# Decoder layer on one core: the last residual sum and the output store of each block in two halves

## The chip, the core and the metric

The kernel runs on one core of a Trainium2 chip. The core has five engines that run side by side, each with a queue of its own: TensorE (PE; its weight loads are listed apart as PEld), VectorE (DVE), ScalarE (ACT), GpSimd (POOL) and SyncE (SP), which here only issues transfers. They wait for each other through semaphores. What counts is the device time of one launch in microseconds (us).

## What is computed

A decoder layer on x of 4 x 1024 tokens with 256 features, in float32. Cut to what matters:

```
x = x + mixer(layernorm(x))              # a state-space scan over time, a projection, its own residual
x = x + cross_attention(ctx, ctx, layernorm(x))       # 16 heads, 64 keys
h = silu(s1 * (z @ w1.T)) * (s2 * (z @ w2.T))         # z = layernorm(x), 256 -> 1024
h = gelu(sh1 * (h @ h1.T)); h = gelu(sh2 * (h @ h2.T))
x = x + s3 * (h @ w3.T)                               # 1024 -> 256
```

The change is in the last line: the sum of x and the feed-forward output, and the store of the result.

## The kernel before

The first part (to about 200 us) is the mixer. The second part, which the change touches, goes over the 4096 tokens in 8 blocks of 512 (`NBLK`, `BLK`). Seven of them run in a loop on every engine (`Fori(0, NBLK - 1)`), the eighth is written out behind it. While the feed-forward part of block i is computed, the attention part of block i + 1 is woven into it; the eighth block has no attention part beside it.

A weight matrix stays in SBUF; an activation is kept as a high and a low part (`hi`, `lo`), so that each product is two matmuls of 128x128 by 512 columns. TensorE (line 1094 on) does per block eight groups of gated products (`gated`, line 1057), 16 groups of hidden products (line 1070), two groups with `w3T` (`last`), and `turn_out` (line 1087): eight transposes that bring the output, which lies with features on the partitions in `sg`, back to tokens on the partitions in the PSUM buffer `pair[2]`. The transposes of feature half k = 0 come first, those of k = 1 behind a wait for ScalarE's second evacuation (`o_ev`, line 775). In `pair[2]` token tile m takes the columns m * 256 to (m + 1) * 256, so its first 512 columns are complete when tiles 0 and 1 of k = 1 are turned.

VectorE's order is written out by hand. At the end of a block it computes the low part of the next block's input (`z_lo`, line 884), then waits for `o_t` and for `xr_in` (the residual rows, loaded by SyncE into `xr` a whole block ahead) and adds (line 954). Right behind the add, in the next trip of the loop, come the statistics of the attention part (`stats`, lines 834 to 841) and then the gated product of group 0 (line 918), for which ScalarE has computed `sg` (line 759). TensorE needs that product's semaphore `v_rdy` before gated group 2, since the groups take turns in two PSUM buffers.

SyncE's order in a trip: load `xr` for block i (line 618), store x2 of block i + 1, load the rows and values of block i + 2, store the output of block i (`out_store`, line 620). After the eighth block it waits for the store, and all engines meet at a barrier (line 1320). Behind it a second program stands that runs only for weights that need it; here each engine reads a flag and branches past it.

Of the kernel before, what the change touches and what calls it, by code (L numbers as in the profile page):

```python
# [29 lines left out]
ALU = mybir.AluOpType  # L30
# [12 lines left out]
BLK = 512  # L43
NBLK = TOK // BLK
TPB = BLK // P
EPS = 1e-5
DH = DM // P
# [488 lines left out]
def layer_program(nc, ctx, a, t):  # L536
    m = mixer_parts(nc, ctx, a, t)
    take = {"a": t["zone_a"], "c": t["zone_c"], "d": t["zone_d"], "s": t["zone_s"]}

    def sb(name, shape, where, dt=F32):  # L540
        size = -(-4 * math.prod(shape[1:]) // 32) * 32
        at, take[where] = take[where], take[where] + size
        return nc.alloc_sbuf_tensor_at(name, shape, dt, offset=at)

    def sem(name):
        return ctx.enter_context(nc.semaphore(name))
# [6 lines left out]
    xr = sb("xr", [P, TPB * DM], "c")  # L553
# [16 lines left out]
    warm = sb("warm", [P, 2], "s")  # L570
    bit_row = bits[0:1, 0:P]
    pair, ident, scl = t["pair"], t["ident"], t["scl"]
# [7 lines left out]

    names = ("h2_in", "xbo_in", "mk", "k_rdy", "v_rdy2", "vb0",
             "stat2", "aggr2", "var_rdy", "rstd", "nat_rdy", "nat_t", "x1b", "sc_ps", "mx", "sub", "exped", "summed", "rcp", "p_rdy",
             "p_t", "t_ev", "av", "wo_ps", "x2a", "x2_rdy", "z_hi", "z_lo", "mm", "sg_rdy", "v_rdy", "hi", "lo", "o_ev", "o_t", "fin1", "fin",
             "x1_in", "v_in", "xr_in", "x2_st", "out_st", "step_v2", "step_s2", "checked", "folded", "col_st", "row_in", "flagged", "warm", "step_g2")
    S = {n: sem("f_" + n) for n in names}

    def blk_rows(d, i):
        return d[bass.ds(i, 1)].rearrange("a p m -> (a p) m")
# [7 lines left out]
    @block.sync  # L596
    def _(e):
        m["sync"](e)

        def attn_loads(j):  # L600
            if not (isinstance(j, int) and j == 0):
                e.wait_ge(S["x2_st"], 16 * j)
                e.sem_inc(S["step_s2"], 1)
                e.wait_ge(S["nat_rdy"], 8 * j)
                e.dma_start(x1t[:, :], blk_rows(x1d, j)).then_inc(S["x1_in"], 16)
            e.wait_ge(S["av"], 2 * j)
            seq = j // (T // BLK)
            for d in range(2):
                e.dma_start(vblk[KEYS * d:KEYS * (d + 1), :], a["ctx"][bass.ds(seq, 1)].rearrange("a s d -> (a s) d")).then_inc(S["v_in"], 16)

        def x2_store(j):
            e.wait_ge(S["x2_rdy"], j + 1)
            e.dma_start(blk_rows(x2d, j), x1t[:, :]).then_inc(S["x2_st"], 16)

        def res_load(i):
            e.wait_ge(S["x2_st"], 16 * i + 16)
            e.wait_ge(S["out_st"], 16 * i)
            e.dma_start(xr[:, :], blk_rows(x2d, i)).then_inc(S["xr_in"], 16)

        def out_store(i):  # L620
            e.wait_ge(S["fin"], i + 1)
            e.dma_start(blk_rows(a["out"], i), xr[:, :]).then_inc(S["out_st"], 16)
        e.wait_ge(m["h_scan"], NOCT)
        attn_loads(0)
        e.dma_start(xbo[:, :], a["xb"].partition_broadcast(P)).then_inc(S["xbo_in"], 16)
        for i in range(1, NBLK):
            m["x1_store"](e, i)
        e.wait_ge(m["x1_st"], 16 * (NBLK - 1))
        e.wait_ge(m["w_d"], 80)
        e.dma_start(t["h2"].bitcast(F32), t["dh2"]).then_inc(S["h2_in"], 16)  # L630
        x2_store(0)
        attn_loads(1)
        with e.Fori(0, NBLK - 2) as i:
            res_load(i)
            x2_store(i + 1)
            attn_loads(i + 2)
            out_store(i)
        res_load(NBLK - 2)
        x2_store(NBLK - 1)
        out_store(NBLK - 2)  # L640
        res_load(NBLK - 1)
        e.wait_ge(S["folded"], 2)
        e.dma_start(t["flag_col"], most[:, :]).then_inc(S["col_st"], 16)
        e.wait_ge(S["col_st"], 16)
        e.dma_start(bit_row, t["flag_col"].rearrange("p o -> o p")).then_inc(S["row_in"], 16)
        out_store(NBLK - 1)
        e.wait_ge(S["out_st"], 16 * NBLK)

    @block.gpsimd
    def _(e):  # L650
# [175 lines left out]
    def _(e):  # L826
# [4 lines left out]
        def stats(n):  # L831

            for m in range(TPB):
                e.bn_stats(st[:, m, :], x1t[:, m * DM:(m + 1) * DM]).then_inc(S["stat2"], 1)
            e.wait_ge(S["stat2"], 4 * n + 4)
            e.wait_ge(S["nat_rdy"], 4 * n)
            e.sem_inc(S["step_v2"], 1)
            for m in range(TPB):
                e.bn_aggr(mv[:, m, :], st[:, m, :]).then_inc(S["aggr2"], 1)
            e.wait_ge(S["aggr2"], 4 * n + 4)  # L840
            e.tensor_scalar_add(ve, mv[:, :, 1], EPS).then_inc(S["var_rdy"], 1)  # L841
# [44 lines left out]
        def low(i, n, dst):  # L886

            e.wait_ge(S["hi"], 24 * i + (n + 1))
            e.tensor_tensor(dst[1][:, n % HC, :], vb[:, n % 2, :], dst[0][:, n % HC, :], ALU.subtract).then_inc(S["lo"], 1)  # L889
# [20 lines left out]
        def body(i, attn):  # L910
            j = i + 1
            if attn:
                e.wait_ge(S["x1_in"], 16 * j)
                stats(2 * j)
            for m in range(HC):
                e.wait_ge(S["sg_rdy"], 8 * i + (m + 1))
                e.wait_ge(S["lo"], 24 * i + max(m - 1, 0))
                e.scalar_tensor_tensor(vb[:, m % 2, :], pair[m % 2][:, 512:1024], sc2[:, m:m + 1], sg[:, m % 2, :],  # L918
                                       ALU.mult, ALU.mult).then_inc(S["v_rdy"], 1)
                if m == HC - 1:  # L920
                    e.wait_ge(S["lo"], 24 * i + m - 1)
                    low(i, m - 1, h1)
                    low(i, m, h1)
                if attn and m == 1:
                    normed(2 * j)
            if attn:
                maxima(j, 0)
                shifted(j, 0)
            for s in range(2 * HC):
                low(i, HC + s, h2 if s < HC else h1)  # L930
                if attn and s in TURN and s != TURN[3]:
                    shifted(j, TURN.index(s) + 1)
                if attn and s + 1 in TURN and s + 1 != TURN[3]:
                    maxima(j, TURN.index(s + 1) + 1)
                if attn and s + 2 in TURN:
                    normalised(j, TURN.index(s + 2))
                if attn and s == 13:
                    residual(j)
                    stats(2 * j + 1)
                if attn and s == 14:  # L940
                    normed(2 * j + 1)
                checks = CHECK if attn else LAST_CHECK
                if s in checks:
                    checked(i, checks.index(s))
                if not attn and s == LAST_CHECK[2] + 1:
                    folded()
                if not attn and s == FLAG_AT:
                    e.wait_ge(S["row_in"], 16)
                    e.tensor_reduce(t["flag"][:, :], bit_row, AX.X, ALU.max).then_inc(S["flagged"], 1)
            if attn:  # L950
                z_lo(j)
            e.wait_ge(S["o_t"], i + 1)
            e.wait_ge(S["xr_in"], 16 * i + 16)
            e.tensor_tensor(xr[:, :], pair[2][:, :], xr[:, :], ALU.add).then_inc(S["fin"], 1)
        m["x1_add"](e, 0)
        e.wait_ge(m["x1a"], 1)
        stats(0)
# [29 lines left out]
    def _(e):  # L987
# [18 lines left out]
        def scores(j, u):  # L1006
            if u == 0:
                e.wait_ge(S["t_ev"], 7 * j + 1)
                e.wait_ge(S["k_rdy"], 2 * j + 2)
                if not isinstance(j, int):  # L1010
                    e.wait_ge(S["fin"], j - 1)
            else:
                e.wait_ge(S["sub"], 4 * j + u)
            h = u // 2
            for b in range(2):
                tile = 2 * (u % 2) + b
                for g in range(2):
                    ins = e.matmul(pair[2][:, g * BLK + b * 256:g * BLK + (b + 1) * 256], qa[64 * g:64 * g + 64, h, tile * P:(tile + 1) * P],  # L1018
                                   kblk[64 * g:64 * g + 64, h * 256:(h + 1) * 256], start=True, stop=True)
            ins.then_inc(S["sc_ps"], 1)  # L1020
# [66 lines left out]
        def turn_out(i):  # L1087
            for k in range(DH):
                e.wait_ge(S["o_ev"], 2 * i + (k + 1))
                for m in range(TPB):  # L1090
                    ins = e.transpose(pair[2][:, m * DM + k * P:m * DM + (k + 1) * P], sg[:, k, m * P:(m + 1) * P], ident[:, :])
            ins.then_inc(S["o_t"], 1)

        def body(i, attn):
            j = i + 1
# [273 lines left out]
```

## Time and profile before

| | |
|---|---|
| three timed runs | 1008.23, 1010.57, 1010.67 us; median 1010.57 |
| the profiled execution | 1008.29 us, of which 1006.6 us from first to last instruction (span) |
| TensorE busy | 887.8 us, 88% of the span |
| VectorE busy | 527.2 us, 52% |
| ScalarE busy | 502.6 us, 50% |
| GpSimd busy | 188.1 us, 19% |
| granted TensorE clock | 0.956 of full speed over the span |

All times in the rows below are microseconds from the span's start, unless a column says ns. The profiled execution was one alone; its rows are added up against its own 1008.29 us. In the chain of waits, "issue" is time in which the engine waited for nothing that the profile shows, and a name with q (DVEq) is the engine's sequencer: register work, waits and branches.

### The profile page before, as it was taken

The numbers are of one execution on the slowest core, as the hardware profiler recorded it, in microseconds if no ns is written. First come the engines' busy times: TensorE is split into PE (matmuls) and PEld (weight loads), VectorE is DVE, ScalarE is ACT, GpSimd is POOL, SyncE is SP. The second block draws the span as 40 slices with busy tenths as digits, with TensorE's granted clock in tenths as the row PEclk, the third lists the DMA queues.
The fourth block names the chain that finished last, engine by engine and source line by source line (L and its number), as shares of the span: only waits on it lengthen the run. The fifth ranks groups of instructions, "written<-read, shape, count | busy, mean of one in ns | idle before, by whom it ended". The sixth has DMA issues, their size and how long they took to land.

```text
span 1006.6 us, 15130 instructions
## 1 busy us (share of the span) xinstructions
PE 887.8 (88%) x5570; PEld 702.4 (70%) x5570; DVE 527.2 (52%) x877; ACT 502.6 (50%) x776; POOL 188.1 (19%) x207
## 2 busy tenths in 40 slices
PE   2038679669999999999999999999999999999996
PEld 0038567457787778777877777778777877777884
DVE  7975326455555555455545554556454645463411
ACT  2863514136644664466356635663566356635431
POOL 0864631022002200220022002200220021003000
PEclk9569889779999999999999999999999999999998
DMA  9976672510002000100010001000100020001000
GB/s 285 250 252 198 242 286 85 209 68 1 1 22 68 0 0 21 68 0 0 21 68 0 0 21 68 0 0 21 68 0 0 21 68 0 0 21 42 1 1 23
DMA packets 14632, 62.82 MB, mean 62 GB/s; under 512 B 2739, under 2 KB 4406, under 8 KB 13782
## 3 DMA queue, kind: packets, MB, share of 16 engines
q1 hardware_dynamic: 13862, 60.19, 17.5%
q10 hardware_dynamic: 704, 2.16, 0.7%
q8 instruction: 23, 0.38, 0.2%
q14 instruction: 11, 0.09, 0.0%
q0 software_dynamic: 32, 0.00, 0.0%
HBM read 50.16 MB, written 23.72 MB: 73 GB/s over the span
## 4 chain that ended last, share of the span: by engine, by line
PE 72%; DVE 12%; issue 7%; ACT 4%; DMA 4%; POOL 0%; SPq 0%; DVEq 0%; ACTq 0%; POOLq 0%
PE pair L1070 45%; PE pair L1057 10%; PE pair L1018 3%; DMA vblk<-in_ctx 3%; PE pair L1029 3%; PE pair L1045 2%; PE pair L462 2%; PE pair L995 2%; PE pair L1038 1%; DVE h1lo L889 1%; PE pair L469 1%; DVE tok L395 1%; DVE tok L391 1%; PE pair L527 1%; PE pair L476 1%
## 5 line engine op out<-in xcount | busy, mean ns | idle before, releaser
L1070 PE MATMUL pair<-h1hi,h_turned 128*128 128x512 f32 x512 | 204.7, 400 | 4.1 <-DVE h1lo L889 4.1
L770 ACT ACTIVATE vbuf<-pair,scl 128x512 f32<-128x512 f32 x128 | 87.6, 684 | 237.2 <-PE pair L1070 231.4
L1070 PE MATMUL pair<-h2hi,h_turned 128*128 128x512 f32 x512 | 202.6, 396 | 0.0
L1070 PE MATMUL pair<-h1lo,h_turned 128*128 128x512 f32 x512 | 199.8, 390 | 0.0
L1070 PE MATMUL pair<-h2lo,h_turned 128*128 128x512 f32 x512 | 199.6, 390 | 0.0
L889 DVE TENSOR_TENSOR h1lo<-vbuf,h1hi 128x512 fp32r<-128x512 f32 x80 | 61.8, 780 | 118.8 <-ACT h1hi L771 118.7
L1070 PEld LDWEIGHTS pair<-h1hi,h_turned 128*128 128x128 f32 x512 | 96.1, 188 | 39.7 <-issue 10.5
L1070 PEld LDWEIGHTS pair<-h2hi,h_turned 128*128 128x128 f32 x512 | 96.1, 188 | 25.2 <-issue 5.9
L1057 PE MATMUL pair<-zThi,w_turned 128*128 128x512 f32 x256 | 105.4, 412 | 5.2 <-DVE vbuf L918 2.6
L1070 PEld LDWEIGHTS pair<-h2lo,h_turned 128*128 128x128 f32 x512 | 96.2, 188 | 19.3
L1070 PEld LDWEIGHTS pair<-h1lo,h_turned 128*128 128x128 f32 x512 | 96.2, 188 | 18.6
L889 DVE TENSOR_TENSOR h2lo<-vbuf,h2hi 128x512 fp32r<-128x512 f32 x64 | 44.2, 690 | 123.4 <-ACT h2hi L771 123.4
L1057 PE MATMUL pair<-zTlo,w_turned 128*128 128x512 f32 x256 | 101.5, 397 | 0.0
L667 POOL TENSOR_TENSOR lnv<-lnv 128x4 f32<-128x4 f32 x16 | 16.3, 1016 | 376.3 <-DVE lnv L841 376.2
L725 ACT ACT_TABLE_LOAD x65 | 83.4, 1283 | 1.2
L918 DVE SCALAR_TENSOR_TENSOR vbuf<-pair,scl,sg 128x512 f32<-128x512 f32 x64 | 47.9, 749 | 68.6 <-ACT sg L759 51.5
L759 ACT ACTIVATE sg<-pair,scl 128x512 f32<-128x512 f32 x64 | 44.1, 689 | 67.1 <-PE pair L1057 67.1
L462 PE MATMUL pair<-tok,EE 64*64 64x60 f32 x512 | 38.8, 276 | 41.4 <-DVE tok L391 41.4
L699 POOL TENSOR_TENSOR h1lo<-vbuf,h1hi 128x512 fp32r<-128x512 f32 x48 | 61.9, 1289 | 60.0 <-ACT h1hi L762 60.0
L1057 PEld LDWEIGHTS pair<-zThi,w_turned 128*128 128x128 f32 x256 | 49.0, 191 | 23.8 <-DVE vbuf L918 8.0
L462 PEld LDWEIGHTS pair<-tok,EE 64*64 64x64 f32 x512 | 29.0, 151 | 42.5 <-DVE tok L391 42.3
L1057 PEld LDWEIGHTS pair<-zTlo,w_turned 128*128 128x128 f32 x256 | 49.0, 191 | 9.2
(124 smaller groups left out, 1439.2 us busy)
## 6 DMA issues: line engine op xcount, KB each, us to landing
h_turned<-d_h SPq DMA_DIRECT2D x2, 4096.0 KB, 13.4
tok<-in_xs SPq DMA_DIRECT2D x8, 512.0 KB, 6.3
EE<-alpha_rows SPq DMA_DIRECT2D x16, 256.0 KB, 11.0
xres<-in_x SPq DMA_DIRECT2D x8, 512.0 KB, 4.0
x_rows<-x1t SPq DMA_DIRECT2D x8, 512.0 KB, 2.6
xr<-x_rows SPq DMA_DIRECT2D x8, 512.0 KB, 3.5
out<-xr SPq DMA_DIRECT2D x8, 512.0 KB, 2.7
x_rows<-xres SPq DMA_DIRECT2D x7, 512.0 KB, 2.7
```

The source lines that it names most:

```text
L462: ins = e.matmul(out, EE[L * h:L * h + L, i, :], rhs, start=True, stop=True)
L699: e.tensor_tensor(h1[1][:, m, :], vb[:, m % 2, :], h1[0][:, m, :], ALU.subtract).then_inc(S["lo"], 1)
L725: e.activation(warm[:, 1:2], warm[:, 0:1], function).then_inc(S["warm"], 1)
L759: e.activation(sg[:, m % 2, :], pair[m % 2][:, 0:512], ACT.Silu, scale=sc1[:, m:m + 1]).then_inc(S["sg_rdy"], 1)
L770: e.activation(vb[:, s % 2, :], h_ps[s % 4], ACT.Gelu, scale=sc)
L889: e.tensor_tensor(dst[1][:, n % HC, :], vb[:, n % 2, :], dst[0][:, n % HC, :], ALU.subtract).then_inc(S["lo"], 1)
L918: e.scalar_tensor_tensor(vb[:, m % 2, :], pair[m % 2][:, 512:1024], sc2[:, m:m + 1], sg[:, m % 2, :], ALU.mult, ALU.mult).then_inc(S["v_rd ...
L995: ins = e.transpose(pair[3][:, k * BLK + m * P:k * BLK + (m + 1) * P], nat[:, m, k * P:(k + 1) * P], ident[:, :])
L1018: ins = e.matmul(pair[2][:, g * BLK + b * 256:g * BLK + (b + 1) * 256], qa[64 * g:64 * g + 64, h, tile * P:(tile + 1) * P], kblk[64 * g:64 ...
L1029: ins = e.transpose(pair[3][:, b * BLK + r * P:b * BLK + (r + 1) * P], prob[:, r // 2, c:c + P], ident[:, :])
L1057: ins = e.matmul(pair[m % 2][:, 512 * g:512 * g + 512], w[:, k, m * P:(m + 1) * P], zT[part][:, k * BLK:(k + 1) * BLK], start=(k == 0 and ...
L1070: ins = e.matmul(bank, w[:, k, m * P:(m + 1) * P], src[part][:, k, :], start=(k == 0 and part == 0), stop=(k == HC - 1 and part == 1))
```

## The change

The final add of a block and its output store are done in two halves of 512 columns each. `turn_out` signals `o_t` twice instead of once: after tile 1 and after tile 3 of the second feature half. VectorE waits for the first signal, adds the first 512 columns and signals `fin`, then waits for the second, adds the rest and signals a new semaphore `fin_b`. SyncE stores each half as soon as its semaphore allows, with `out_st` and a new `out_st_b`; the next load into `xr` and the end of the program wait for both. The next block's scores, which overwrite `pair[2]`, wait for `fin_b`. The wait for the residual rows now stands ahead of the wait for the transposes.

```
         def res_load(i):
             e.wait_ge(S["x2_st"], 16 * i + 16)
             e.wait_ge(S["out_st"], 16 * i)
+            e.wait_ge(S["out_st_b"], 16 * i)
             e.dma_start(xr[:, :], blk_rows(x2d, i)).then_inc(S["xr_in"], 16)
 
         def out_store(i):
-            e.wait_ge(S["fin"], i + 1)
-            e.dma_start(blk_rows(a["out"], i), xr[:, :]).then_inc(S["out_st"], 16)
+            for k in range(2):
+                e.wait_ge(S[("fin", "fin_b")[k]], i + 1)
+                e.dma_start(blk_rows(a["out"], i)[:, k * BLK:(k + 1) * BLK], xr[:, k * BLK:(k + 1) * BLK]).then_inc(S[("out_st", "out_st_b")[k]], 16)
...
         out_store(NBLK - 1)
         e.wait_ge(S["out_st"], 16 * NBLK)
+        e.wait_ge(S["out_st_b"], 16 * NBLK)
...
-            e.wait_ge(S["o_t"], i + 1)
             e.wait_ge(S["xr_in"], 16 * i + 16)
-            e.tensor_tensor(xr[:, :], pair[2][:, :], xr[:, :], ALU.add).then_inc(S["fin"], 1)
+            for k in range(2):
+                here = slice(k * BLK, (k + 1) * BLK)
+                e.wait_ge(S["o_t"], 2 * i + (k + 1))
+                e.tensor_tensor(xr[:, here], pair[2][:, here], xr[:, here], ALU.add).then_inc(S[("fin", "fin_b")[k]], 1)
...
                 if not isinstance(j, int):
-                    e.wait_ge(S["fin"], j - 1)
+                    e.wait_ge(S["fin_b"], j - 1)
...
                 for m in range(TPB):
                     ins = e.transpose(pair[2][:, m * DM + k * P:m * DM + (k + 1) * P], sg[:, k, m * P:(m + 1) * P], ident[:, :])
-            ins.then_inc(S["o_t"], 1)
+                    if k == DH - 1 and m % 2 == 1:
+                        ins.then_inc(S["o_t"], 1)
```

How the instructions stand: VectorE, the end of a loop trip, before. ISA is an instruction of the sequencer alone, here a wait.

```order
L889 TENSOR_TENSOR h1lo<-vbuf,h1hi 128x512 [waits f_hi]
L884 TENSOR_TENSOR zTlo<-pair,zThi 128x1024 [waits f_z_hi]
L953 ISA [waits f_o_t]
L954 TENSOR_TENSOR xr<-pair,xr 128x1024 [waits f_xr_in]
L982 REGISTER_ALU
L982 COMPARE_AND_BRANCH
```

The same place after the change:

```order
L892 TENSOR_TENSOR h1lo<-vbuf,h1hi 128x512 [waits f_hi]
L887 TENSOR_TENSOR zTlo<-pair,zThi 128x1024 [waits f_z_hi]
L955 ISA
L958 ISA [waits f_xr_in]
L959 TENSOR_TENSOR xr<-pair,xr 128x512 [waits f_o_t]
L958 REGISTER_ALU
L959 TENSOR_TENSOR xr<-pair,xr 128x512 [waits f_o_t]
L987 REGISTER_ALU
L987 COMPARE_AND_BRANCH
```

The wait for the transposes (`f_o_t`) moved from an instruction of its own onto the adds, and the wait for the loaded rows took its place; the trip has three instructions more.

SyncE, from the last x2 store to the end of the program (the barrier follows its last wait), before:

```order
L613 DMA x_rows<-x1t 128x1024 [waits f_x2_rdy]
L622 DMA out<-xr 128x1024 [waits f_fin]
L618 DMA xr<-x_rows 128x1024 [waits f_out_st,f_x2_st]
L643 DMA flag_column<-most 128x1 [waits f_folded]
L645 DMA bits<-flag_column 1x128 [waits f_col_st]
L622 DMA out<-xr 128x1024 [waits f_fin]
L1320 UNCONDITIONAL_BRANCH [waits f_out_st]
```

And after:

```order
L613 DMA x_rows<-x1t 128x1024 [waits f_x2_rdy]
L624 DMA out<-xr 128x512 [waits f_fin]
L624 DMA out<-xr 128x512 [waits f_fin_b]
L619 DMA xr<-x_rows 128x1024 [waits f_out_st_b,f_out_st,f_x2_st]
L645 DMA flag_column<-most 128x1 [waits f_folded]
L647 DMA bits<-flag_column 1x128 [waits f_col_st]
L624 DMA out<-xr 128x512 [waits f_fin]
L624 DMA out<-xr 128x512 [waits f_fin_b]
L1326 UNCONDITIONAL_BRANCH [waits f_out_st_b,f_out_st]
```

Each output store became two, the second behind a wait of its own, and what follows them waits for both.

## Rows read from the trace of the kernel before

**Rows 1.** Page, chain that ended last: share of the span by engine

```profile
PE 72%; DVE 12%; issue 7%; ACT 4%; DMA 4%; POOL 0%; SPq 0%; DVEq 0%; ACTq 0%; POOLq 0%
```

**Rows 2.** Chain in order of time, 814 to 823.9 us: start, us, what

```profile
814.29 0.67 PE pair L1091 x4
814.96 0.03 issue
814.99 0.05 DVEq L953
815.04 0.05 issue
815.09 0.07 DVE xr L954
...
815.79 0.43 issue
816.23 1.40 DVE st L834 x4
...
818.42 0.76 DVE vbuf L918
819.18 0.04 issue
819.23 3.93 PE pair L1057 x16
```

**Rows 3.** Waits, borders near 815 and 915: us in total, times, longest

```profile
PEld pair L1057 <- DVE vbuf L918: 0.8, 1, 0.8
PE pair L1057 <- DVE vbuf L918: 0.4, 1, 0.4
...
PEld pair L1057 <- DVE vbuf L918: 0.2, 1, 0.2
```

**Rows 4.** Timeline 808 to 834: start, us, engine, line, out<-in [idle before <-releaser]

```profile
817.12 0.69 ACT L759 ACTIVATE sg<-pair,scl 128x512 f32<-128x512 f32 x1 [1.38 <-PE pair L1057]
818.43 0.39 PE L1057 MATMUL pair<-zTlo,w_turned 128*128 128x512 f32 x1
819.23 0.50 PE L1057 MATMUL pair<-zThi,w_turned 128*128 128x512 f32 x1 [0.41 <-DVE vbuf L918]
820.25 2.30 DVE L847 TENSOR_SCALAR nat<-x1t,mv,lnv 128x256 f32<-128x256 f32 x4
822.76 1.03 PEld L995 LDWEIGHTS pair<-ident,nat 128*128 128x128 f32 x8
823.00 1.04 PE L995 MATMUL pair<-ident,nat 128*128 128x128 f32 x8
```

**Rows 5.** Durations: ns min/median/max by line; the last two from groups (busy, mean)

```profile
L1091 PE MATMUL pair<-ident,sg x64: 272/273/332, 312.0 to 996.7; 128*128 128x128 f32 x64
...
L954 DVE TENSOR_TENSOR xr<-pair,xr 128x1024 f32<-128x1024 f32 x8 | 9.8, 1224 | 27.1 <-PE pair L1091 27.1
...
L889 DVE TENSOR_TENSOR h2lo<-vbuf,h2hi 128x512 fp32r<-128x512 f32 x64 | 44.2, 690 | 123.4 <-ACT h2hi L771 123.4
```

**Rows 6.** End: chain's last step of issue, and timeline's store on SyncE's queue

```profile
997.00 0.02 issue
...
998.27 0.36 SPq L622 DMA_DIRECT2D out<-xr  x1
```

**Rows 7.** Lines 889 and 858, 834 to 837 us: ns, first and last start

```profile
L889 DVE TENSOR_TENSOR h1lo<-vbuf,h1hi x2: 1219/1226/1232, 834.4 to 835.5; 128x512 fp32r<-128x512 f32 x2
...
L858 DVEq FUSED_REGOPS  x1: 46/46/46, 835.2 to 835.2; - x1
```

**Rows 8.** Stretches of last store: us, five engines busy, PEclk, DMA share, GB/s

```profile
998.27:999.13 0.86, 0.00 (x0) 0.00 (x0) 0.00 (x0) 0.00 (x0) 0.00 (x0) 1.00 0.00 0
999.13:1000.43 1.30, 0.00 (x0) 0.00 (x0) 0.00 (x0) 0.00 (x0) 0.00 (x0) 1.00 0.99 403
```

**Rows 9.** SyncE's queue behind its wait for the last store (line 1320)

```profile
L1320 SPq COMPARE_BRANCH  x1: 38/38/38, 1001.0 to 1001.0; - x1
```

**Rows 10.** DMA queues from 320 to 915 us, and TensorE's last branch (ns)

```profile
q1 hardware_dynamic: 3909, 11.95, 5.5%
...
L1251 PEldq COMPARE_BRANCH  x1: 3876/3876/3876, 1002.3 to 1002.3; - x1
```

## What I expect of the change, and why

> **What bounds the kernel now.** I read the page first, for who is busy and who ends the chain: TensorE holds 72% of the chain that ended last and VectorE 12% [rows 1]. So the final sum, a VectorE operation, can matter only where VectorE is in that 12%. I then followed the chain of waits across a border between two blocks, where this sum stands. It reads the same at six borders (near 314, 414, 514, 615, 715 and 815 us); rows 2 are the last. The four transposes of the output's second half run from 814.29 to 814.96, the sum (line 954) starts at 815.09, behind it on VectorE the statistics of the next block start at 816.23, then the first gated product (line 918) at 818.42, and only its end at 819.18 lets TensorE's third gated group go at 819.23 [rows 2]. So **the sum is on the path at six borders**. TensorE's price there: the weight load waits 0.8 us and the matmuls 0.4 us [rows 3]. Counted in starts, the matmul before begins at 818.43 and the next could follow 0.23 later, at 818.66 (the pace of that line), but begins at 819.23: 0.57 us lost [rows 4]. At the seventh border (near 915 us) the next block has no attention part and no statistics, and the same wait is 0.2 us of weight load and nothing of the matmuls [rows 3]: nothing to win. After the last block the sum and the store end the kernel: all that lies on them counts in full.
>
> **What the change does at a border.** (1) The semaphore fires after the second of the four transposes. Four take 0.67 us; the first of a burst takes 0.33 and each later one (0.67 - 0.33) / 3 = 0.11 more, so two are done after 0.44 [rows 2, 5]. Gain 0.22 us. (2) Today the loop's wait on the transposes is an instruction of its own: end of transpose 814.96, that wait 814.99, sum 815.09, so 0.13 us from releaser to sum; at the kernel's end, where the sum carries the wait itself, the same step takes 0.02 [rows 2, 6]. In the new order (above) the half sum carries it in the loop too, and the wait for the loaded rows, long done, takes the separate place. Gain 0.11 us. (3) One sum of 1024 columns takes 1.224 us; a tensor operation of 512 columns takes 0.690 [rows 5]. Sum and statistics overlap by 0.08 (815.09 + 1.224 = 816.31 against 816.23) [rows 2], and I let the two halves overlap alike: 2 x 0.69 - 0.08 = 1.30, a loss of 0.08 us. The second half never waits: the first runs from about 814.76, the last transpose ends at 814.96. Net 0.22 + 0.11 - 0.08 = **0.25 us, times six borders 1.5 us**.
>
> Does the shift arrive? The first gated product would start at 818.17; its other input, ScalarE's operation at 817.12, is done at 817.81 [rows 4]. 0.25 is under the 0.57 that TensorE loses. Next late is the transpose of the normalised rows: these are ready at 820.25 + 2.30 = 822.55 and do not move, since they hang on the second gated product. Their weight load starts at 822.76 and the first matmul at 823.00 [rows 4]: 0.21 us are free, and up to 0.45 while only the load slips. So 0.25 passes, 0.21 if not.
>
> Bounds for one border. From above 0.33: the second half costs nothing extra. From below 0.10, if the register work and the branch behind the sum begin only when the second half starts: today that work runs from the sum's start to 815.79, 0.70 us, hidden by the sum (0.43 us are left over) [rows 2]; behind a second half at 815.37 it ends at 816.07, and the statistics start about 816.13. If the second half also paid a separate wait of 0.11, the gain would be about nothing, which is the end below. I take 0.25, since the queue is seen to run ahead: of two 512-column subtractions at 834.4 and 835.5, the register operation behind the second (line 858) runs at 835.2, before the second starts [rows 7].
>
> The Trainium skill ("VectorE: DVE Perf Modes", the section on the TRN2 errata) speaks against the split: each instruction pays a fixed latency, so many small tiles pay it many times, and an fp32 add takes (N + 151) / 0.96 ns, which is 691 ns for 512. The trace agrees with that duration (690) [rows 5] but shows 0.08 of it overlapped; without that overlap a border would gain 0.17 and all six 1.0, as an estimate from that page.
>
> **What it does at the end.** No separate wait goes there, so the sum gains 0.22 - 0.08 = 0.14 us. The store today is issued at 998.27, its packets run from 999.13 to 1000.43 (1.30 us at 403 GB/s), and SyncE goes on at about 1000.98 (the row rounds to 1001.0) [rows 6, 8, 9]. Two stores of 256 KB move for 0.65 us each. The first half is summed by about 997.5 and its packets run 998.38 to 999.03; the second is issued at 998.13, 0.14 before today's, its packets start at 998.99, wait 0.04 behind the first, and end near 999.68; 0.55 later, at 1000.23, SyncE goes on. Gain 0.75. Bounds: 0.14 if a half lands as late as a whole, 0.79 without the wait. SyncE pays one more issue, 0.35 us, over by 997.9 and so covered by the second half sum. From 1000.98 to the end nothing changes.
>
> **What costs nothing.** TensorE signals once more in a row of transposes; a matmul that signals is followed at the usual pace. In the loop SyncE issues one more store and waits once more; the next load into these rows is needed 95 us later. The scores now wait on the second semaphore, long signalled.
>
> **Sum:** 1.5 + 0.75 = 2.25 us. Against the profiled run of 1008.29 that is 1006.0; against the median, 1010.57 - 2.25 = **1008.3**. The profiled run lies at the low end of the three timed ones, which are 2.4 us apart, more than the change is worth.
>
> **Rivals.**
> - The queue does not run ahead over the second half: 6 x 0.10 + 0.75 = 1.35, 1009.2. For: a third instruction is then pending on the queue with the branch behind it. Against: rows 7.
> - The halves do not hasten the store, 6 x 0.25 + 0.14 = 1.64, 1008.9. For: only 1.30 of 2.71 us is transfer. Against: that 1.30 is at 0.99 busy engines [rows 8], so it goes with the bytes.
> - The borders give nothing (a separate wait at both halves, or a next wait that takes it all): 0.75, 1009.8. Against: the 0.21 free at the transpose.
> - Slower: VectorE's loop, three instructions longer, no longer stays in what its sequencer keeps, and each trip fetches code. Today no code is fetched from 320 to 915 us: only the data queue has packets [rows 10]. A branch that lands on absent code took 3.88 us at the end [rows 10]; at six borders that is 23 us, 1032. It decides as soon as one fetch shows per trip; nothing says that three instructions reach it.
>
> **Chances.** The forecast 0.62, the queue 0.15, the store 0.10, nothing at the borders 0.09, slower 0.04. A measurement can tell about 0.3%, 3.0 us, from no change, and no case but the last moves that far by itself. But if the median of the runs after falls to the low end of the spread, where one of three timed runs and the profiled one lie, it reads 1006 to 1007, over 0.3% below 1010.57; I give that 0.3 of 0.96. So faster 0.29, same 0.67, slower 0.04. Range: from 1008.29 with the upper bounds, 6 x 0.33 + 0.79 = 2.8, so 1005.5, to the median with the store alone, 1009.8, with a little for spread 1010.0.
>
> **What would show it.** At a border: the first half starts about 0.33 us before today's sum against the transposes' start, the statistics 0.25 earlier, the weight load's wait falls from 0.8 to 0.6 us, and the border-to-border time (near 100 us) shrinks by 0.25. At the end: last store issued 0.14 earlier, then 2.1 us to SyncE's going on. If the halves stand apart by 0.69 instead of 0.61, or the statistics start 0.7 us or more after the second half, step (3) is wrong; code packets in the loop mean the slower case.

## The result: 2.6 us faster, under what counts as clear

| | before | changed |
|---|---|---|
| median of 20 timed runs each | 1009.41 us (1005.0 to 1011.9) | 1006.73 us (1002.59 to 1009.57) |
| ratio | | 0.9974, 95% interval 0.9962 to 0.9986 |
| profiled execution, span | 1006.6 us | 1007.8 us |

The ratio is a gain of 2.6 us (1.4 to 3.8), 0.26%; 2.25 us were forecast. The span of the profiled execution points the other way, so spans alone mislead here: the changed kernel's profiled execution, 1009.57 us, was the slowest of its twenty. The difference lies ahead of the changed code: the first border's transposes start at 312.95 in the profile of before and at 316.64 in that of the changed kernel, and across all kernels below that start falls anywhere from 311.9 to 316.6 us. From there on the traces are steady to some hundredths, with one exception (the last block of experiment 1), and the reading goes by differences from the start of the burst of transposes. A trip here is the time from one such burst to the next.

The chain of waits of the changed kernel at the first and at the sixth border (start, us, what), to be held against rows 2:

```profile
316.64 0.46 PE pair L1096 x2
...
816.74 0.46 PE pair L1096 x2
817.20 0.02 issue
817.22 0.05 DVE xr L959
...
817.58 0.25 issue
817.83 0.07 DVE xr L959
817.89 0.16 issue
818.05 0.06 DVEq L838
818.12 0.31 issue
818.43 1.41 DVE st L837 x4
...
820.62 0.76 DVE vbuf L921
821.38 0.04 issue
821.43 3.93 PE pair L1062 x16
```

The chain leaves the burst after two transposes, not four. Measured from the burst's start: the sum starts at 0.48 (before 0.80), the second half at 1.09, the statistics at 1.69 (before 1.94), TensorE goes on at 4.69 (before 4.94). The first sum is 0.32 us early, and of that 0.25 us is left at the statistics and at TensorE. The five trips between the two borders take (816.74 - 316.64) / 5 = 100.02 us. In the profile of before the first border reads

```profile
312.95 0.67 PE pair L1091 x4
```

and the sixth 814.29 [rows 2], which makes 100.27. **The trips are 0.25 us shorter**; from the first burst to the last burst, in the eighth block, 683.4 became 681.9 us.

The weight load's wait at the border, and the stores of the last block on SyncE's queue with the sum ahead of them (timeline), and SyncE going on:

```profile
PEld pair L1062 <- DVE vbuf L921: 0.6, 1, 0.6
```

```profile
998.51 0.65 PE L1096 MATMUL pair<-ident,sg 128*128 128x128 f32 x4 [0.34 <-ACT sg L778]
999.06 1.29 DVE L959 TENSOR_TENSOR xr<-pair,xr 128x512 f32<-128x512 f32 x2 [6.55 <-PE pair L1096]
999.78 0.94 SPq L624 DMA_DIRECT2D out<-xr  x2
```

```profile
L1326 SPq COMPARE_BRANCH  x1: 38/38/38, 1002.6 to 1002.6; - x1
```

The wait fell from 0.8 [rows 3] to 0.6 us. At the end SyncE goes on 4.65 us after the burst starts in before (996.33 to 1000.98) and 4.07 in the changed kernel: 0.58 won, against 0.75 forecast. The rest of the tail is read in experiments 3, 4 and 8.

### The profile page after: what moved, and what is told of

Same layout as the page of the kernel before. It is cut to its first block, busy times and chain, and to the rows that moved or that the text cites. A ratio compares the mean times of both kernels' runs of the same rounds, so it can differ in the third digit from the quotient of the medians.

```text
span 1007.8 us, 15173 instructions
## 1 busy us (share of the span) xinstructions
PE 888.6 (88%) x5570; PEld 703.5 (70%) x5570; DVE 528.1 (52%) x885; ACT 502.8 (50%) x776; POOL 188.1 (19%) x207
## 4 chain that ended last, share of the span: by engine, by line
PE 72%; DVE 14%; issue 7%; ACT 3%; DMA 3%; POOL 1%; DVEq 0%; SPq 0%; ACTq 0%; POOLq 0%
PE pair L1075 45%; PE pair L1062 10%; PE pair L1023 3%; PE pair L1034 3%; DMA vblk<-in_ctx 3%; PE pair L1050 2%; PE pair L462 2%; PE pair L1000 2%; PE pair L1043 1%; DVE h1lo L892 1%; PE pair L469 1%; DVE st L382 1%; PE pair L476 1%; DVE tok L395 1%; DVE tok L391 1%
```

## Experiments

Experiments 1 to 4, 7 and 8 are one profiled execution each. Their total times say little beside the spread of the start, so they are read from the trace alone. Three of these kernels have the loop of before: before itself and experiments 4 and 7. Their mean trips are 100.27, 100.28 and 100.29 us, so a difference of 0.03 in a mean trip shows nothing by itself.

**1. The wait's form alone.** In the kernel before:

```
-            e.wait_ge(S["o_t"], i + 1)
             e.wait_ge(S["xr_in"], 16 * i + 16)
+            e.wait_ge(S["o_t"], i + 1)
             e.tensor_tensor(xr[:, :], pair[2][:, :], xr[:, :], ALU.add).then_inc(S["fin"], 1)
```

> The kernel before with one edit: the wait for the loaded rows stands ahead of the wait for the transposes, so that the whole sum carries the latter itself. Only step (2) of the prediction. My theory (three steps add up: 0.22 earlier signal, 0.11 wait form, 0.08 lost to a second instruction): last transpose to sum falls from 0.13 to about 0.02 us, the statistics start 0.11 earlier, and each of the six trips near 100.25 us shortens by 0.11; the end is unchanged. Rival (what shortens the trips is the signal alone, and the wait form is an effect of how rows are drawn): trips unchanged at 100.25.

Measured: trips of (815.69 - 314.36) / 5 = 100.27 us, as before, and the statistics only 0.03 us earlier (1.91 after the burst). The chain at the fifth border says why:

```profile
715.43 0.67 PE pair L1091 x4
716.10 0.03 issue
716.13 0.02 DVEq L953
716.15 0.04 issue
716.19 0.07 DVE xr L954
```

The edit did not do what I meant. The wait for the transposes is still an instruction of the sequencer (line 953), only a lighter one: 0.09 us from the transposes' end to the sum, where [rows 2] have 0.13. So this run tests nothing of a wait on the sum itself; it gives a third row for the price of a wait. In the changed kernel the half sum does carry it, and follows the second transpose by 0.02 us (817.20 to 817.22). The end, expected unchanged, is 0.05 us later: there the transposes' wait had been on the sum, and the swap made it a separate instruction, so the sum starts 0.07 later. The stretch from the seventh border to the last burst took 82.14 us, where the other kernels have 81.7 to 81.8, and nothing in this edit explains it.

**2. Two half sums behind the late signal.** As 1, and

```
-            e.tensor_tensor(xr[:, :], pair[2][:, :], xr[:, :], ALU.add).then_inc(S["fin"], 1)
+            e.tensor_tensor(xr[:, 0:BLK], pair[2][:, 0:BLK], xr[:, 0:BLK], ALU.add)
+            e.tensor_tensor(xr[:, BLK:2 * BLK], pair[2][:, BLK:2 * BLK], xr[:, BLK:2 * BLK], ALU.add).then_inc(S["fin"], 1)
```

> The kernel before with the wait order of the first experiment, and the sum in two halves that both follow the signal of the last transpose; one store. Steps (2) and (3) without (1). My theory: against before 0.11 gained and 0.08 lost, so trips of 100.22 us (0.03 shorter than before, 0.08 longer than in the first experiment), the second half 0.61 behind the first. Rival (a second instruction pays its full 0.157 us): trips 0.05 longer than before. At the end the store is issued 0.08 later than before.

Measured: trips of (816.77 - 315.27) / 5 = 100.30 us, 0.03 longer than in experiment 1 and than before, which is what equal loops differ by. The forecast was 0.03 shorter than before: the wait's form brought 0.03 instead of 0.11 again. The price of the halving is clear in the chain, the same at all six borders:

```profile
716.47 0.67 PE pair L1092 x4
...
717.24 0.10 DVE xr L954
...
717.84 0.13 DVE xr L955
717.97 0.47 issue
718.44 1.40 DVE st L834 x4
```

The halves start 0.60 apart and the statistics start 1.97 after the burst, 0.07 later than in experiment 1 (717.33 - 715.43 = 1.90). Step (3) put it at 0.08; the full 0.157 of a second instruction is excluded. So halving without an early signal costs time. At the end the store is issued 0.13 us later than before, where 0.08 was expected: 0.07 for the swapped waits and 0.06 for the halving.

**3. The split sum with one store.** The changed kernel, with

```
-            for k in range(2):
-                e.wait_ge(S[("fin", "fin_b")[k]], i + 1)
-                e.dma_start(blk_rows(a["out"], i)[:, k * BLK:(k + 1) * BLK], xr[:, k * BLK:(k + 1) * BLK]).then_inc(S[("out_st", "out_st_b")[k]], 16)
+            e.wait_ge(S["fin_b"], i + 1)
+            e.dma_start(blk_rows(a["out"], i), xr[:, :]).then_inc(S["out_st"], 16)
...
```

> The changed kernel with one store of 512 KB behind the second half's sum. All of the border steps, nothing of the store. My theory: trips of 100.0 us as in the changed kernel, and at the end 2.7 us from the store's issue to SyncE's going on as before, so the tail gains only what the sum gains (0.05 to 0.14 us). Rival (the second store in the loop costs or brings something at the borders): trips other than 100.0.

Measured: trips of (812.27 - 312.25) / 5 = 100.00 us. The whole gain of the border is in the sum and its signal; the second store brings and costs nothing there that these traces can tell. The end:

```profile
994.58 1.29 DVE L956 TENSOR_TENSOR xr<-pair,xr 128x512 f32<-128x512 f32 x2 [6.55 <-PE pair L1093]
995.90 0.36 SPq L622 DMA_DIRECT2D out<-xr  x1
```

```profile
L1323 SPq COMPARE_BRANCH  x1: 38/38/38, 998.6 to 998.6; - x1
```

2.7 us from issue to going on, as before [rows 6, 9]. SyncE goes on 4.54 after the burst: 0.11 of the tail's 0.58 is the sum, the rest the second store.

**4. Only the last block.** The kernel before, whose eighth block alone signals twice, sums in halves and stores in halves (here the wait for the transposes stands first). VectorE's part of the edit:

```
...
+            else:
+                for k in range(2):
+                    here = slice(k * BLK, (k + 1) * BLK)
+                    e.wait_ge(S["o_t"], i + 1 + k)
+                    if k == 0:
+                        e.wait_ge(S["xr_in"], 16 * i + 16)
+                    e.tensor_tensor(xr[:, here], pair[2][:, here], xr[:, here], ALU.add).then_inc(S[("fin", "fin_b")[k]], 1)
...
```

> The kernel before in its loop; only the eighth block has two signals, two half sums and two stores. My theory: trips of 100.25 us as before; at the end the last store lands 2.1 us after its issue, SyncE goes on about 4.0 us after the last burst of transposes starts, where before it is 4.65; 0.6 us in all. The sum carries the wait for the transposes itself here, so the first half should start about 0.07 us sooner than in the changed kernel's last block. Rival (the tail gain of the changed kernel is chance in the last branch): 4.65 as before.

Measured: trips of (814.88 - 313.48) / 5 = 100.28 us. SyncE goes on 3.99 after the burst, 0.66 earlier than in the kernel before. The first half starts 0.07 earlier than in the changed kernel's last block, where the order of the waits had made the one for the transposes an instruction of its own again. The two parts of the change are thus apart: borders 1.5 us, end 0.6 us.

**5. The sum taken off the border.** The changed kernel; on VectorE the half sums of block i - 1, with their waits (`summed_out`), move into trip i, and the first block, which has no block ahead of it, is written out in front of the loop:

```
...
+                if late and m == 3:
+                    summed_out(i - 1)
...
-        with e.Fori(0, NBLK - 1) as i:
+        body(0, True, False)
+        with e.Fori(1, NBLK - 1) as i:
```

> The changed kernel with the two half sums of a block moved on VectorE from the border into the next trip, behind the gated product of group 3, where VectorE is idle for 1.97 us; the eighth block sums at its end as in the changed kernel. Takes the sum off the path and asks how much was to be had at a border. My theory: the statistics start right behind the low part of the next input, the first gated product as soon as ScalarE's input is there (about 0.3 us earlier than in the changed kernel), TensorE's 0.57 us stall goes, trips fall from 100.0 to 99.6 or 99.7 us, and at six borders 2 us are saved over the changed kernel (about 4 to 4.5 us, 0.4%, against before). Rival A (the next wait, the transpose of the normalised rows, is late by 0.2 us and takes the rest): trips of 99.8. Rival B (the sum at its new place delays the product of group 4 and TensorE's group 6 with it): trips of 100.0 or more.

Measured: median 1006.65 us, ratio to before 0.9974 (0.9960 to 0.9988), no better than the changed kernel. The trip behind the first border took 411.59 - 312.34 = 99.25 us, the four next (812.77 - 411.59) / 4 = 100.30. The late sum stands in every one of them, in the first too:

```profile
322.43 1.28 DVE L919 TENSOR_TENSOR xr<-pair,xr 128x512 f32<-128x512 f32 x2
```

So it is not the late sum that parts 99.25 from 100.30. TensorE's stall at the border was gone in all of them (it goes on at 4.42 after the burst, at its own pace), and in all but the first the gain was lost 4 us later. The timeline of VectorE and of GpSimd near the sixth border, and TensorE's wait (the same at the fifth and the sixth):

```profile
818.01 0.75 DVE L929 SCALAR_TENSOR_TENSOR vbuf<-pair,scl,sg 128x512 f32<-128x512 f32 x1 [0.89 <-ACT sg L762]
818.68 3.36 DVE L850 TENSOR_SCALAR nat<-x1t,mv,lnv 128x256 f32<-128x256 f32 x4
```

```profile
818.57 1.30 POOL L702 TENSOR_TENSOR h1lo<-vbuf,h1hi 128x512 fp32r<-128x512 f32 x1 [4.74 <-ACT h1hi L765]
820.61 1.27 POOL L702 TENSOR_TENSOR h1lo<-vbuf,h1hi 128x512 fp32r<-128x512 f32 x1 [0.74 <-ACT h1hi L765]
```

```profile
PEld pair L1008 <- DVE nat L850: 1.4, 1, 1.4
```

The four normalising operations take 3.36 us here, 2.30 in before [rows 4]. Their durations at the fifth border and at the first (ns min/median/max), and GpSimd's second subtraction at the first:

```profile
L850 DVE TENSOR_SCALAR nat<-x1t,mv,lnv x4: 400/873/1447, 718.4 to 720.3; 128x256 f32<-128x256 f32 x4
...
L850 DVE TENSOR_SCALAR nat<-x1t,mv,lnv x4: 400/400/1325, 318.3 to 320.2; 128x256 f32<-128x256 f32 x4
```

```profile
320.24 1.49 POOL L702 TENSOR_TENSOR h1lo<-vbuf,h1hi 128x512 fp32r<-128x512 f32 x1 [0.77 <-ACT h1hi L765]
```

In every trip the first of the four meets GpSimd's first subtraction and lasts 1.3 instead of 0.4 us; this is so in before too. What is new is the second subtraction. In before it starts 8.37 us after the burst, when the four are done. With TensorE half a microsecond ahead it starts at 7.84 to 7.90 after the burst, within 0.06 us of the fourth operation. Then one of the two is held up: at the first border it is GpSimd's (1.49 instead of 1.28 us, and the fourth takes 0.40), at the other five VectorE's (1.45 to 1.47 us, and TensorE waits 1 us). Between the two outcomes the starts differ by hundredths, and why the first border fell the other way stays open. Rival A was right in kind (the transposes of these rows are next late) and wrong in size, since I had counted on the rows staying where they were. The Trainium skill ("SBUF — State Buffer", the section on the two separate sides) tells of a port pair that VectorE and GpSimd share and that one of them holds for a whole instruction; these rows agree that one waits for the other. They don't show that the earlier start decides: the recorded start of the fourth operation is ahead of the subtraction's in the cases that it lost as well.

**6. The normalising operations moved to where GpSimd is idle.** Experiment 5, and

```
...
                 stats(2 * j)
+                normed(2 * j)
...
-                if attn and m == 1:
-                    normed(2 * j)
...
```

> The fifth experiment's kernel with one more move on VectorE: the four normalising operations of the next block's attention (line 850 there) stand right behind the statistics, ahead of the gated product of group 0, where VectorE was idle for 3.65 us, instead of behind the product of group 1. My theory for why the fifth experiment gained nothing (trips of 99.25 us once, then 100.3): with TensorE half a microsecond ahead, GpSimd's second low part starts before the last of the four normalising operations, that one takes 1.4 instead of 0.4 us beside it, the transposes of these rows wait for it and TensorE with them. Then here, with GpSimd idle beside them, all four take 1.4 us in all, the transposes do not wait, and every trip is 99.2 to 99.3 us or less: 6 us against before with the end's 0.6, about 1002 us where before reads 1008.6. Rival (the late sum itself, ahead of the product of group 4, costs the microsecond): trips of 100 or more as in the fifth experiment.

Measured: **median 999.22 us, ratio to before 0.9901 (0.9887 to 0.9916)**, 10 us faster, and every trip (807.37 - 311.87) / 5 = 99.10 us. The late sum is still in each trip, so it was not what cost experiment 5 its gain. Beside an idle GpSimd the four operations, near the fifth border, read

```profile
L850 DVE TENSOR_SCALAR nat<-x1t,mv,lnv x4: 405/406/411, 709.4 to 710.3; 128x256 f32<-128x256 f32 x4
```

Of the 1.17 us per trip 0.57 is the stall at the border. About 0.4 appears where the gated groups end and the hidden ones begin: two low parts of VectorE, 2.38 us in before, take 1.83 beside GpSimd's additions on the next block's rows, and TensorE's wait for them shrinks. The rows of this kernel, and that wait behind the first border in before and in experiment 5:

```profile
727.73 1.83 DVE L892 TENSOR_TENSOR h1lo<-vbuf,h1hi 128x512 fp32r<-128x512 f32 x2
```

```profile
PE pair L1070 <- DVE h1lo L889: 0.6, 2, 0.4
```

```profile
PE pair L1083 <- DVE h1lo L892: 0.2, 1, 0.2
```

I had not foreseen that part. It is in experiment 5 already, in its first trip and in the later ones alike (1.83 us from 331.96, 1.82 from 432.27), so it came with the late sum and not with the moved operations. GpSimd's four additions take 3.76 us there instead of 3.28: again the two engines changed places, one of VectorE's low parts going free (0.68 instead of 1.22 us) and one addition being held. What the moved operations bring is that the meeting of experiment 5 no longer happens: against that kernel's first trip 0.15 us, against the others 1.2. No run moves them without the late sum, so what they are worth alone is not shown.

From the first burst to the last, 7.0 of the 10 us are seen in the trace and 1.0 behind the last burst; the start varies too much for one profile to say where the other 2 are, and the interval begins at 8.5.

**7. The last block in quarters.** Experiment 4 with four sums and four stores of 256 columns, two behind each signal. SyncE's part, as far as its waits go:

```
...
-        for k in range(2):
-            e.wait_ge(S[("fin", "fin_b")[k]], (NBLK, 1)[k])
+        for k in range(4):
+            e.wait_ge(S[("fin", "fin_b", "fin_c", "fin_d")[k]], (NBLK, 1, 1, 1)[k])
...
```

> The fourth experiment's kernel with the last block summed and stored in four quarters of 256 columns, two behind each signal. My theory (a store is fixed time plus its bytes, and a sum is 0.157 us plus its columns, overlapped by 0.08): quarter sums of 0.42 us, 0.35 apart, so the last ends 0.1 later than the last half did; the last store has a fourth of the bytes, 0.33 instead of 0.65 us, so SyncE goes on 0.1 to 0.2 us sooner than in the fourth experiment (3.8 to 3.9 us after the last burst of transposes instead of 3.99). Rival (stores queue up behind each other, by issue or by a fixed cost each): 4.3 us or more.

Measured: SyncE goes on 4.4 us after the burst (1003.1 against a burst at 998.70), 0.4 later than with halves. Both rows:

```profile
999.17 1.42 DVE L968 TENSOR_TENSOR xr<-pair,xr 128x256 f32<-128x256 f32 x4 [6.49 <-PE pair L1105]
999.62 1.82 SPq L648 DMA_DIRECT2D out<-xr  x4
```

```profile
L1336 SPq COMPARE_BRANCH  x1: 43/43/43, 1003.1 to 1003.1; - x1
```

The sums came as expected (four in 1.42 us, done at 1000.59), but SyncE needs 1.82 us to issue four stores (0.36 for the first, 0.43 to 0.45 for the others) and is done only at 1001.44. Issue is the bound, which my sum for quarters left out: from the first packet to the last, 1000.49 to 1002.48, the DMA engines were busy for only 77% of the time. With two stores 0.35 us of issue still fits under the second half sum.

**8. The changed kernel again.**

> The changed kernel once more, for a second profile. The borders and the end repeat to 0.03 us (trips of 100.0; SyncE goes on 4.07 after the last burst starts). TensorE's last branch was 3.88, 4.00, 3.52 and 3.92 us in the kernels with one last store and 3.46, 3.36 and 3.46 with two. If the change shortens it, it is 3.4 to 3.5 here again; if it is chance, it may lie anywhere from 3.4 to 4.0.

Measured: trips of (814.48 - 314.49) / 5 = 100.00 us; SyncE goes on 4.06 after the last burst. TensorE's last branch took

```profile
L1257 PEldq COMPARE_BRANCH  x1: 3521/3521/3521, 1001.7 to 1001.7; - x1
```

3.52 us, like experiment 2, which has one store. So the 0.4 us between 3.88 in before [rows 10] and 3.46 in the first profile of the changed kernel is not shown to belong to the change. Two stores gave 3.36 to 3.54 us in five profiles, one store 3.52 to 4.00 in four. The four stores of experiment 7 gave 3.62. A small effect isn't excluded, and it stays open.

## Why the prediction was right, step by step

- **Where it counts.** Six borders and the end: borne out. At the seventh border nothing moved (81.78 and 81.74 us from there to the eighth block's burst).
- **(1) and (2), the earlier start.** 0.22 + 0.11 = 0.33 forecast, 0.32 measured (0.48 against 0.80 after the burst starts). That (2) is worth its 0.1 in the loop rests on two rows, 0.13 us from transpose to sum in before and 0.02 in the changed kernel; the experiment meant to isolate it did not.
- **(3), the second instruction.** 0.08 forecast, 0.07 measured (experiment 2).
- **The shift arrives.** 0.25 per trip forecast and measured, 1.5 us over six borders. The queue ran ahead over the second half: in the chain above the branch work stands ahead of 817.83. The transposes of the normalised rows, with 0.21 us free by my count, did not wait. Experiment 5 shows what a shift of 0.5 meets: not these free 0.21 us, but GpSimd's second subtraction, on which the prediction has no word.
- **The end, the term that was mis-sized.** 0.75 forecast, 0.58 measured. The step that failed is the sentence that no separate wait goes there and the sum gains 0.14: in the constant code of the last block the swapped waits did become a separate one, which costs 0.07 (experiments 3 and 4), so the last store is issued 0.08 earlier. From issue to going on the stores gained 0.50 against 0.61; 0.06 of that gap is a second wait on SyncE. The other 0.05 is in the transfer, which I had taken to go with the bytes alone. The packets of before and of the changed kernel's last stores:

```profile
DMA packets 144, 0.52 MB, mean 187 GB/s; under 512 B 16, under 2 KB 16, under 8 KB 144
```

```profile
DMA packets 288, 0.52 MB, mean 181 GB/s; under 512 B 32, under 2 KB 32, under 8 KB 288
```

  The same bytes went in twice as many packets, and from the first packet to the last both halves took 1.52 us (1000.64 to 1002.16) where the whole took 1.43 (999.14 to 1000.57).
- **The rivals.** Queue, stores and borders are each refuted by the traces. The timed gain alone would not part them: the store rival's 1.64 us lies in 1.4 to 3.8, and the queue rival's 1.35 just outside. The slower case too: from 320 to 915 us the changed kernel's trace has packets on the data queue alone:

```profile
q1 hardware_dynamic: 4733, 12.25, 5.8%
```

- **The measurement.** 1.5 + 0.6 = 2.1 us are shown in the traces, the timed 2.6 has an interval of 1.4 to 3.8. The fear that a median of few runs would land at the low end of the spread was about noise and not about the change; with 20 runs each it played no part. The absolute forecast, 1008.3 us, was 1.6 above the 1006.73 measured, and 1.2 of that is its starting point: the median of three runs was 1010.57, that of twenty 1009.41. That 1006.73 still lies in the stated range owes something to luck, since the range's lower end was counted from the one profiled run, 1008.29, and not from the median. That nothing changes behind SyncE's going on is not shown either way (experiment 8).

## What to carry to other kernels

An operation that is off the bottleneck engine can still be on the path where two stages meet: read the chain at the border, count how long the bottleneck waits there, and multiply by the trips. Splitting it paid here together with an earlier signal; alone it cost 0.07 us a border. Before moving VectorE work, and before moving TensorE ahead in time, look at what GpSimd will do then: taking the sum off the path won 1 us in one trip and nothing in the others, and only with four short operations out of GpSimd's way as well did it win in every trip, 1% of the kernel.

## What the runs showed of the hardware

- A wait on a semaphore costs by its form: carried by the waiting vector operation 0.02 us from releaser to start, as an instruction of its own with a constant or ready value 0.09 to 0.10, with a register computation in it 0.13.
- VectorE's normalising operations of 0.4 us last 1.3 to 1.5 us each when they meet a GpSimd subtraction of 1.3 us. A shift of half a microsecond elsewhere brought two starts within 0.06 us of each other; which engine then waited differed between trips of one run, and a whole gain with it (99.25 against 100.30 us).
- Stores of one DMA each took 0.34 to 0.36 us of SyncE's queue alone or in a pair, and in a row of four 0.43 to 0.45 from the second on, though each had fewer bytes.
- From issue to going on, a store of 512 KB took 2.7 us and the second of two of 256 KB 2.2. The same 512 KB took 1.43 us from first to last packet in 128 packets of 4096 bytes and 1.52 in 256 of 2048.
